# A nine-expert MoE kernel on one core: down products taken one and two chunks late, both prefix casts moved up on ScalarE, the up sum and h kept in one SBUF tile

## The reference

```python
def _L0_cond_ref(hidden_states, gating_probs, shared_gate_prob, Wg, Wu, Wd, Sg, Su, Sd):
    E, B, S, D, F = (8, 2, 256, 256, 1024)
    h = hidden_states
    g = jnp.einsum('bsd,edf->ebsf', h, Wg)
    u = jnp.einsum('bsd,edf->ebsf', h, Wu)
    expert_outs = jnp.einsum('ebsf,efd->ebsd', jax.nn.silu(g) * u, Wd)
    expert_output = jnp.einsum('be,ebsd->bsd', gating_probs, expert_outs)
    shared = jnp.einsum('bsf,fd->bsd', jax.nn.silu(h @ Sg) * (h @ Su), Sd)
    sg = shared_gate_prob[:, :, None]
    return (1.0 - sg) * expert_output + sg * shared
x = x + _L0_cond_ref(x, fside_Bx8_0, condB_sharedgateprob[:, None], ...)
```

## Time and profile before

| | us |
|---|---|
| median of 3 runs | 2305.16 (2304.65 to 2307.76) |
| the profiled execution's own time | 2306.76 |
| its span, first to last instruction | 2305.0 |
| PE busy | 2246.9 (97%) |
| DVE busy | 1802.1 (78%) |
| POOL busy | 1651.5 (72%) |
| ACT busy | 1430.8 (62%) |

### The profile page before, as it was taken

One profiled execution on the slowest core, in us unless ns is written; L12 is line 12 of the kernel. 1 busy time (PEld: TensorE's weight loads), 2 busy tenths in 40 slices (PEclk: granted clock), 3 DMA queues, 4 the chain that ended last, 5 costly groups with the idle time before them and its releaser, 6 DMA issues.

```text
span 2305.0 us, 33781 instructions
## 1 busy us (share of the span) xinstructions
PE 2246.9 (97%) x9504; PEld 1765.6 (77%) x9504; DVE 1802.1 (78%) x2622; ACT 1430.8 (62%) x2334; POOL 1651.5 (72%) x2055
## 2 busy tenths in 40 slices
PE   6999999999999999999999999999999999999998
PEld 4777777777777777777777777777777777777776
DVE  6777777777777777777777777777778778777787
ACT  5666666666666666666666666666666666666664
POOL 7877777777887767767787677677676677677663
PEclk9999999999999999999999999999999999999999
DMA  4111111111111111111121111111112111111110
GB/s 136 55 48 55 48 48 55 48 48 55 60 56 48 52 51 48 51 51 48 50 64 56 48 48 55 48 48 55 48 48 67 55 48 48 54 48 49 54 48 25
DMA packets 44170, 122.21 MB, mean 53 GB/s; under 512 B 4928, under 2 KB 4944, under 8 KB 44128
## 3 DMA queue, kind: packets, MB, share of 16 engines
q1 hardware_dynamic: 44064, 121.65, 17.1%
q0 software_dynamic: 64, 0.07, 0.1%
HBM read 117.51 MB, written 4.19 MB: 53 GB/s over the span
## 4 chain that ended last, share of the span: by engine, by line
PE 49%; DVE 25%; issue 16%; ACT 8%; DVEq 1%; ACTq 1%; DMA 0%; SPq 0%; POOL 0%
DVE h L422 16%; PE chain_ps L256 9%; DVE up L450 8%; ACT tap_p L353 7%; PE chain_ps L258 6%; PE down_ps L256 6%; PE down_ps L258 6%; PE chain_ps L257 6%; PE down_ps L257 6%; PE p_ps L256 3%; PE p_ps L257 3%; PE p_ps L258 3%; DVEq L118 0%; ACTq L118 0%; DMA acc<-xT 0%
## 5 line engine op out<-in xcount | busy, mean ns | idle before, releaser
L183 POOL TENSOR_TENSOR w_lo<-w_raw,w_hi 128x384 fp32r<-128x384 f32 x864 | 912.1, 1085 | 593.9 <-ACT w_hi L323 593.8
L345 ACT CAST h_hi<-h 128x512 fp32r<-128x512 f32 x576 | 361.4, 627 | 658.1 <-DVE h L422 653.1
L168 POOL TENSOR_TENSOR w_raw<-w_raw 128x128 f32<-128x128 f32 x1152 | 700.6, 628 | 33.6 <-DMA acc<-xT 8.8
L422 DVE SCALAR_TENSOR_TENSOR h<-silu,coef,up 128x256 f32<-128x256 f32 x576 | 607.6, 1093 | 32.7 <-DVE up L450 7.5
L256 PE MATMUL chain_ps<-x_hi,w_hi 128*128 128x512 f32 x1152 | 480.0, 417 | 44.1 <-POOL w_lo L183 20.1
L444 DVE TENSOR_TENSOR gate<-tap_u,p_ps 128x512 f32<-128x512 f32 x288 | 198.0, 687 | 397.6 <-PE p_ps L258 397.6
L256 PE MATMUL down_ps<-h_hi,w_hi 128*128 128x512 f32 x1152 | 452.0, 392 | 8.3 <-DVE h_lo L430 8.3
L257 PE MATMUL chain_ps<-x_lo,w_hi 128*128 128x512 f32 x1152 | 450.6, 391 | 0.0
L258 PE MATMUL chain_ps<-x_hi,w_lo 128*128 128x512 f32 x1152 | 450.6, 391 | 0.0
L258 PE MATMUL down_ps<-h_hi,w_lo 128*128 128x512 f32 x1152 | 449.8, 390 | 0.0
L257 PE MATMUL down_ps<-h_lo,w_hi 128*128 128x512 f32 x1152 | 449.2, 390 | 0.0
(11 more groups left out here) (38 smaller groups left out, 2125.8 us busy)
## 6 DMA issues: line engine op xcount, KB each, us to landing
w_raw<-w SPq DMA_DIRECT2D x288, 384.0 KB, 3.0
outT<-acc SPq DMA_DIRECT2D x8, 512.0 KB, 4.7
acc<-xT SPq DMA_DIRECT2D x6, 512.0 KB, 9.2
acc<-xT SPq DMA_DIRECT2D x4, 256.0 KB, 6.2
probs_sb<-probs POOLq DMA_DIRECT2D x1, 64.0 KB, 5.3
shared_sb<-shared_gate POOLq DMA_DIRECT2D x1, 8.0 KB, 6.5
```

Of the source, the lines that this page charges most:

```text
L168: nc.gpsimd.tensor_tensor(raw[:, cols(dst, dst)], raw[:, cols(a, a)], raw[:, cols(b, b)], op).then_inc(w_sums, 1)
L183: ins = nc.gpsimd.tensor_tensor(w_lo[:, s, c], w_raw[:, s, c], w_hi[:, s, c].bitcast(F32), ALU.subtract)
L345: nc.scalar.copy(h_hi[:, t], h[:, t]).then_inc(h_hi_done[t], 1)
L422: ins = nc.vector.scalar_tensor_tensor(h[:, 1, s], silu[:, 1, s], coef_of(g, e, 1, half), up1[:, s], ALU.mult, ALU.mult)
```

## The change

On PE the p4 of a unit is issued at the head of the next unit. Tile 0's down product is issued two units late (`down0`, between p5 and p6), tile 1's one unit late (`down1`, at the unit's end). Tile 0's `h_hi` and `h_lo` are doubled for it. On ACT, the cast of the weights is split into 768 and 384 columns, both placed around `tap_u2` and ahead of the two silus; the casts for the next group's x stand there too; and h1's cast moves to the head of the next unit. On DVE, h1's low part now comes first in the next unit, before h0, and h0's low part comes before gate0. h1 is written over `up1`, in place. The two adds at a group's end are spread over two units. POOL's wait for the next group's x moves to its first use.

The core of the diff:

```diff
             def weight_lo(n, s):
-                pool.wait_ge(w_hi_done, n + 1)
+                pool.wait_ge(w_hi_done, 2 * (n + 1))
...
                 if form == T1:
+                    pool.wait_ge(pair_loaded[g - 1], 32)
...
+                if not isinstance(n, int) or n > 0:
+                    p4(g - 1 if first else g, (k - 1) % CHUNKS, n - 1, first=in_first and k == 1)
                 pe.wait_ge(w_lo_done, n + 1)
                 after(pe, h0_done, n - 1)
-                product(chain, s, A11, *x(B11), start=True, stop=True).then_inc(p1_done, 1)
+                product(chain, s, A11, *x_of(g, B11, first), start=True, stop=True).then_inc(p1_done, 1)
                 after(pe, gate1_done, n)
-                product(p53_ps[:], s, S1, *x(T1), start=True, stop=True).then_inc(p5_done, 1)
+                product(p53_ps[:], s, S1, *x_of(g, T1, first), start=True, stop=True).then_inc(p5_done, 1)
+                if not isinstance(n, int) or n > 1:
+                    pe.wait_ge(h_lo_done[0], n - 1)
...
+                    down0((k - 2) % CHUNKS, start=opens, stop=in_first and k == 1)
+                pe.wait_ge(p1_tapped, n + 1)
+                product(chain, s, S2, *x_of(g, T2, first), start=False, stop=True, goes_on=True).then_inc(p6_done, 1)
                 after(pe, gate0_done, n)
-                product(p2_ps[:], s, A12, *x(B21), start=True, stop=True).then_inc(p2_done, 1)
+                product(p2_ps[:], s, A12, *x_of(g, B21, first), start=True, stop=True).then_inc(p2_done, 1)
...
+                    down1((k - 1) % CHUNKS, start=opens, stop=first)
...
         def _(act):
-            def weight_hi(n, s):
+            def weight_hi(n, s, part):
                 act.wait_ge(w_sums, 4 * (n + 1))
                 after(act, down_done[0], n - SLOTS + 1)
-                nc.scalar.copy(w_hi[:, s, :], w_raw[:, s, :]).then_inc(w_hi_done, 1)
+                c = slice(0, S1 * P) if part == 0 else slice(S1 * P, FORMS * P)
+                nc.scalar.copy(w_hi[:, s, c], w_raw[:, s, c]).then_inc(w_hi_done, 1)
...
+                if not first:
+                    h1_hi_of(n - 1)
                 act.wait_ge(p1_done, n + 1)
...
                 if not first:
-                    h_hi_of(0, n - 1, h0_done)
+                    h0_hi_of(n - 1, k - 1)
+                if ahead:
+                    weight_hi(n + AHEAD, (k + AHEAD) % SLOTS, 0)
                 act.wait_ge(p6_done, n + 1)
                 after(act, gate1_done, n)
                 nc.scalar.copy(tap_u2[:], chain_ps[:, k % 2, :]).then_inc(u2_tapped, 1)
+                if ahead:
+                    weight_hi(n + AHEAD, (k + AHEAD) % SLOTS, 1)
+                if new_x:
+                    for form in X_AT.get(k, ()):
+                        x_form_hi(g + 1, form)
                 act.wait_ge(gate0_done, n + 1)
                 after(act, h0_done, n)
                 nc.scalar.activation(silu[:, 0], gate[:, 0], ACT.Silu).then_inc(silu_done[0], 1)
-                if not isinstance(n, int) or n + AHEAD <= LAST:
-                    weight_hi(n + AHEAD, (k + AHEAD) % SLOTS)
...
                 nc.scalar.activation(silu[:, 1], gate[:, 1], ACT.Silu).then_inc(silu_done[1], 1)
-                h_hi_of(1, n, h1_done)
...
-                after(dve, h_lo_done[1], n)
                 for half in range(HALVES):
                     s = half_of(half)
                     ins = nc.vector.scalar_tensor_tensor(
-                        h[:, 1, s], silu[:, 1, s], coef_of(g, e, 1, half), up1[:, s], ALU.mult, ALU.mult
+                        up1[:, s], silu[:, 1, s], coef_of(g, e, 1, half), up1[:, s], ALU.mult, ALU.mult
                     )
...
                 if before[0] >= 0:
-                    h0(*before, n - 1)
-                    h_lo_of(1, n - 1)
+                    h1_lo_of(n - 1)
+                    h0_of(*before, n - 1)
+                    h0_lo_of(n - 1, k - 1)
                 gate0(n)
-                if before[0] >= 0:
-                    h_lo_of(0, n - 1)
                 gate1(n)
                 up_of_1(n, k)
                 h1(g, e, n)
-                if closes and before[0] >= 0:
-                    for t in (1, 0):
-                        add(before[0], t, n - 1)
+                if isinstance(e, int) and e == 0 and g > 0:
+                    if k == 0:
+                        add(g - 1, 1, n - 1)
+                    if k == 1:
+                        add(g - 1, 0, n - 2)
```

More of the change, by code:

```diff
@@ L57, in moe_kernel @@
         gate = sb("gate", [P, 2, TOKENS])
+        silu = sb("silu", [P, 2, TOKENS])
         up1 = sb("up1", [P, TOKENS])
[L59 to L62, removed]
+        h0 = sb("h0", [P, TOKENS])
+        h0_hi = sb("h0_hi", [P, 2, TOKENS], F32R)
+        h0_lo = sb("h0_lo", [P, 2, TOKENS], F32R)
+        h1_hi = sb("h1_hi", [P, TOKENS], F32R)
+        h1_lo = sb("h1_lo", [P, TOKENS], F32R)
         probs_sb = sb("probs_sb", [P, BATCH, ROUTED])
@@ L258, in product, with x_of, down0, down1 @@
                 return nc.tensor.matmul(bank, w_lo[:, s, c], hi, start=False, stop=stop, **on)
-            def down(g, k, t, start, stop):
+            def x_of(g, form, first):
+                if first:
+                    pe.wait_ge(x_lo_done, X_FORMS * g + form + 1)
+                return x_hi[:, g % 2, form, :], x_lo[:, g % 2, form, :]
+            def down0(k, start, stop):
                 for c in range(DC):
                     last = product(
-                        down_ps[:, t, c, :], k % SLOTS, D0 + c, h_hi[:, t, :], h_lo[:, t, :], start, stop
+                        down_ps[:, 0, c, :], k % SLOTS, D0 + c, h0_hi[:, k % 2, :], h0_lo[:, k % 2, :], start, stop
                     )
-                last.then_inc(down_done[t], 1)
-            def unit(g, e, k, first=False):
+                last.then_inc(down_done[0], 1)
+            def down1(k, start, stop):
+                for c in range(DC):
+                    last = product(down_ps[:, 1, c, :], k % SLOTS, D0 + c, h1_hi[:], h1_lo[:], start, stop)
+                last.then_inc(down_done[1], 1)
+            def p4(g, k, n, first=False):
+                pe.wait_ge(up1_done, n + 1)
+                x = x_of(g, T4, first)
+                product(chain_ps[:, k % 2, :], k % SLOTS, A22, *x, start=False, stop=True, goes_on=True).then_inc(
+                    p4_done, 1
+                )
+            def unit(g, e, k):
                 n = g * PER + e * CHUNKS + k
@@ L271, in unit @@
                 chain = chain_ps[:, k % 2, :]
[L273 to L280, removed]
+                in_first = isinstance(e, int) and e == 0
@@ L287, in unit @@
-                after(pe, gate0_done, n)
-                product(p2_ps[:], s, A12, *x(B21), start=True, stop=True).then_inc(p2_done, 1)
-                pe.wait_ge(p1_tapped, n + 1)
-                product(chain, s, S2, *x(T2), start=False, stop=True, goes_on=True).then_inc(p6_done, 1)
+                product(p53_ps[:], s, S1, *x_of(g, T1, first), start=True, stop=True).then_inc(p5_done, 1)
+                if not isinstance(n, int) or n > 1:
+                    pe.wait_ge(h_lo_done[0], n - 1)
+                    opens = in_first and k == 2
+                    if opens:
+                        after(pe, added[0], g)
+                    down0((k - 2) % CHUNKS, start=opens, stop=in_first and k == 1)
@@ L291, in unit @@
+                product(chain, s, S3, *x_of(g, T3, first), start=False, stop=True, goes_on=True).then_inc(p7_done, 1)
                 if not isinstance(n, int) or n > 0:
                     pe.wait_ge(h_lo_done[1], n)
[L293 to L306, removed]
+                    opens = in_first and k == 1
@@ L308, in _ @@
+                    if opens:
+                        after(pe, added[1], g)
+                    down1((k - 1) % CHUNKS, start=opens, stop=first)
             for g in range(GROUPS):
                 for k in range(CHUNKS):
-                    unit(g, 0, k, first=(k == 0))
+                    unit(g, 0, k)
                 with pe.Fori(1, EXPERTS) as e:
@@ L349, in unit @@
                 first = isinstance(n, int) and n == 0
+                ahead = not isinstance(n, int) or n + AHEAD <= LAST
+                if not first:
+                    h1_hi_of(n - 1)
                 act.wait_ge(p1_done, n + 1)
@@ L422, in h1, with h0_lo_of, h1_lo_of @@
                     ins = nc.vector.scalar_tensor_tensor(
-                        h[:, 1, s], silu[:, 1, s], coef_of(g, e, 1, half), up1[:, s], ALU.mult, ALU.mult
+                        up1[:, s], silu[:, 1, s], coef_of(g, e, 1, half), up1[:, s], ALU.mult, ALU.mult
                     )
                 ins.then_inc(h1_done, 1)
[L427 to L431, removed]
+            def h0_lo_of(n, k):
+                dve.wait_ge(h_hi_done[0], n + 1)
+                after(dve, down_done[0], n - 1)
+                nc.vector.tensor_tensor(
+                    h0_lo[:, k % 2], h0[:], h0_hi[:, k % 2].bitcast(F32), ALU.subtract
```

(8 more changed lines are left out.)

51 lines of the change are left out of this document (30 added, 21 removed).

## The result

| | median us | ratio to the kernel before, 95% interval |
|---|---|---|
| before, in the same rounds | 2306.46 (2304.65 to 2307.81, 4 runs) | 1 |
| changed | 2355.03 (2350.91 to 2358.09, 4 runs) | 1.0210 (1.0188 to 1.0232) |

The change made the kernel 2.1% slower; the forecast was 2341 us, 1.5%, with a range of 2302 to 2376. The profiled execution took 2350.91 us, with a span of 2349.1 against 2305.0: 44.1 us more. It is the fastest of the four, 4.1 us under their median, so sums of its trace are compared with 44.1 us and not with the difference of the medians. Of the runs in this document one is left out, a run of 3680.70 us of the kernel with h1 in a tile of its own, at a granted clock of 0.558 where all others had 0.997 to 1.

What follows compares the result with a forecast made beforehand. The prediction took a loop through ACT, DVE and POOL, closed by h1 and w_lo taking turns at the SBUF port, as the bound. Sum: 2306.8 + 26 (loop) + 9 (x) - 4 (adds) + 3 (race) = 2340.8 us; range 2302 to 2376.

Steps and rivals of the forecast that it cites:

- the race: DVE's h1_lo against POOL's third weight sum for the SBUF port; a loss costs 0.32 us, one in thirty units, 3 us.
- The group starts: Next group's x: POOL's x_lo delays h1_lo, 0.5 us in each of 18 units, 9 us; adds spread over two units, -4.
- The bound: Loop through ACT, DVE and POOL, 7.86 us a unit, against PE's own floor of 7.48; PE's tap_p1 wait only shows it.
- the turns of h1 and w_lo: DVE's two h1 and POOL's three w_lo alternate at the SBUF port; h1 ends 3.43 us after w_lo starts.
- The new loop's length: From h1's end to h1's end through ACT, DVE and POOL: 7.96 us against 7.86, 26 us over some 264 units.
- Rival 1: h1_lo loses the port race often: every third unit 25 us more, 2366 us; every unit, 2422; chance 0.13.
- h1 in place costs nothing: DVE's h1 written over up1: both inputs in SBUF as before, so the turns with w_lo stay, 3.43 us.
- PE gets a stall at p7, some 0.3 us: On PE, p7 waits for tap_u2 in nearly every unit, some 0.3 us, replacing the wait for tap_p1.
- Rival 2: h1 slips between first and second w_lo, turns break, PE bounds at 7.48 us: 109 us off, 2198 us; chance 0.12.

## Why the prediction was right

The mechanism was right and its main term came out; the sum was 10 us short, 34 against 44.1, because of one term, the race. The group starts came out near by two errors that cancel.

- *The bound*, a loop through ACT, DVE and POOL closed by the turns of h1 and w_lo: right, and shown. Breaking the turns, by a wait or by the place of the cast (2192 and 2193 us in the changed kernel, 2200 and 2202 in the one before), or shortening the rest of the loop (2190), gave PE's 7.48 to 7.50 us.
- *The new loop's length*, 7.96 us: measured 7.95. The two casts, forecast 0.83 and 0.52, took 0.83 and 0.51. 7.952 - 7.859 = 0.093 us over 285 units is 26.5 us of the 44.1, forecast 26.
- *The race*, "at one in thirty units it is 3 us": the term that was mis-sized. The long units away from the group starts add 22.5 us, and two things are in them. Ties were lost 33 times of 232, one in seven, 11 us. That rate could have been read more nearly in the kernel before: of its 263 h_lo that started within 0.03 us of a weight sum, 25 lost, one in eleven, which at the forecast's own 0.32 us makes 8 us, not 3. The other 12 us stand in the 29 last units of the loop rounds, for which the sum had nothing; holding the sum back took 4 us of these and all 11 of the ties. Rival 1, the race lost in one unit of three, put 28 us there: by the time lost it came nearer than my sum, though the ties alone are one in seven.
- *The group starts*, 9 - 4 = 5 us: measured -1 (9.1 us over the loop before, 8.2 now), and both terms were off. The first two units of groups 1 to 3 were 10.1 us over the loop before and are 2.6 over it now, 7.5 us off where I took 4, though that the adds alone do it was not tested. The other first units of groups 0 to 2 cost 6.6 us more, where I took 9: x_lo held h1_lo in three units each of groups 1 and 2 (1.00 to 1.02 us).
- *The start of the run*, which I had at nothing: the first tap_u2 comes 2.9 us earlier, at 22.6 against 25.6. By the trace PE's first product starts 1.7 us sooner, at 18.39 against 20.06, and p6 stands one product (1.3 us) further forward.
- Sum: 26.5 + 22.5 - 0.9 - 2.9 = 45.2 us; the last two units and the tail take 1.2 off, which leaves 44.0 of the 44.1.
- *h1 in place costs nothing*: the loop is 7.95 us with and without it. *PE gets a stall at p7, some 0.3 us*: 0.28 us, in 269 units.
- *Rival 2*, PE bounds at 7.48 and 2198 us: not what this change does, and within 8 us what its neighbours do. The forecast said that h1 came 0.4 us too late; it starts at 1015.30, the second w_lo 0.39 us ahead of it. With the whole cast behind both silus w_lo comes after h1, and the rival's 7.48 us are there.
- Not separated: PE's new order was never undone by itself. That its cure leaves the changed kernel 8 us ahead of the cured kernel before is all that the runs say of it, and some 2.5 us of that are the earlier first tap_u2.

## What to carry to other kernels

When the busiest engine waits a little in every round, follow the loop through the other engines' lists until it closes, and compare its length with the engine's own: the wait's name is only where it shows. Here the named wait went away and the loop was 0.09 us longer, while swapping two calls on DVE in the changed kernel, or moving one cast on ACT in either, gave a kernel some 5% faster than the kernel before. Two instructions that exclude each other tie their engines' phases together; putting the start of the one behind the end of the other can be worth more than making either shorter, even if it adds a wait.

## What the runs showed of the hardware

The race for the port isn't decided by the recorded starts: with h1_lo 0.02 us ahead it won at 752.66 and lost at 760.62. The rate differed between programs: of the ties within 0.03 us the VectorE instruction lost 33 of 232 in the changed kernel and 7 of 232 with h1 in a tile of its own, which has the same loop. In the kernel before it lost 25 of 263, although in nearly all of them its recorded start was up to 0.013 us behind GpSimd's. The Trainium skill (SBUF — State Buffer, Who interferes with whom) gives the port to the one that issues first. The profile records starts and not issues; by the recorded starts the second of the two pairs doesn't agree, and the measurement decides.

An h1_lo that lost took 1.02 us instead of 0.69. A pair of h1 that took turns with the three w_lo took 1.78, 2.07, 2.14 or 2.42 us in the median, depending on where it started, instead of 0.88. What stayed the same is its end: 3.43 us after the first w_lo's start, in the median of each of the six kernels with turns. The pair of h0, with its second factor in PSUM, took 0.86 to 0.87 in the median of every kernel.
